# Layer 1's end rearranged: the dense experts' weights in the bias strips' space, batch 6's experts begun earlier, the last head group's tiles two per step

## The reference, cut to what matters

```python
x = x + ga * attn(layernorm(x) * (1 + ca) + sa)        # 16 heads, position bias: "attention 0"
h = layernorm(x) * (1 + cb) + sb
h = h + mla(rmsnorm(h, g1))                            # causal, 16 heads: "attention 1"
t = rmsnorm(h, g2)
top_v, top_i = top_k(t @ gate_w, 2)                    # 8 experts, two per token
gates = softmax(top_v)
hid = silu(einsum('td,edh->teh', t, w1))               # 128 -> 256, each expert
ye = einsum('teh,ehd->ted', hid, w2)                   # 256 -> 128
h = h + sum over the token's two experts of gate * ye
x = x + gb * h
```

## Time and profile before

| | |
|---|---|
| median of 3 runs | 1876.62 us (1873.95 to 1883.99) |
| profiled execution, its own time | 1871.64 us |
| its span, first to last instruction | 1869.9 us |
| mean granted clock of TensorE | 0.947 |
| PE, DVE, ACT, POOL busy | 87%, 71%, 54%, 42% |

### The profile page before, as it was taken

The page is one execution under the profiler, slowest core; times in us unless marked ns, Lnnn a source line. Parts: engine busy times, 40 slices in busy tenths (PEclk is TensorE's granted clock), DMA queues, the critical chain, the costliest instruction groups (busy, mean ns, idle before and its releaser), DMA issues.

```text
span 1869.9 us, 50554 instructions
## 1 busy us (share of the span) xinstructions
PE 1622.4 (87%) x19264; PEld 1184.4 (63%) x19264; DVE 1324.6 (71%) x4176; ACT 1008.1 (54%) x2196; POOL 778.9 (42%) x1021
## 2 busy tenths in 40 slices
PE   3889898899883939999999999989999989878887
PEld 2667776777772727766666666757767667534545
DVE  6678767876761127788778898897877886475646
ACT  1555454555451316665666766656666666454542
POOL 3111211220115237786656576565564563434120
PEclk7899999999995969999999999999999999888999
DMA  4631122122004424344423324243443233535421
GB/s 117 182 94 46 40 84 61 39 69 82 5 8 127 151 91 147 127 151 158 151 85 110 122 96 151 75 142 91 140 142 103 99 126 116 156 95 148 121 64 53
DMA packets 143839, 194.53 MB, mean 104 GB/s; under 512 B 21920, under 2 KB 110176, under 8 KB 142320
## 3 DMA queue, kind: packets, MB, share of 16 engines
q1 hardware_dynamic: 129312, 171.75, 29.5%
q0 software_dynamic: 5760, 14.03, 2.3%
q10 hardware_dynamic: 8528, 5.51, 1.0%
HBM read 142.39 MB, written 50.69 MB: 103 GB/s over the span
## 4 chain that ended last, share of the span: by engine, by line
PE 44%; DVE 10%; issue 6%; ACT 5%; DMA 2%; POOL 1%; SPq 0%; ACTq 0%; another core or an unknown queue 0%; POOLq 0%; DVEq 0%
PE ps L2350 9%; PE ps L2333 7%; PE ps L2384 6%; PE ps L2394 3%; DVE l_XY L2601 3%; PE ps L2361 3%; PE ps L2484 2%; PE ps L2459 2%; ACT PT L2162 2%; DVE ps L2601 2%; PE ps L1229 2%; PE ps L1238 2%; PE ps L2410 1%; PE ps L2431 1%; PE ps L2363 1%
## 5 line engine op out<-in xcount | busy, mean ns | idle before, releaser
L2053 POOL TENSOR_SCALAR l_XY<-l_XY,l_nmax 128x512 f32<-128x512 f32 x512 | 374.3, 736 | 301.7 <-DVE l_nmax L2601 293.5
L2601 DVE CUSTOM_DVE_ANT_0 l_XY<-ps,strips 128x512 f32<-128x512 f32 x512 | 348.0, 687 | 173.4 <-PE ps L2333 115.2
L2162 ACT ACTIVATE PT<-ps 128x512 f32<-128x512 f32 x512 | 307.5, 601 | 244.6 <-PE ps L2350 236.0
L2333 PE MATMUL ps<-l_stack 72*128 72x512 bf16 (+3 forms) x1024 | 351.4, 348 | 54.4 <-DVE l_nmax L2601 39.9
L2350 PE MATMUL ps<-ident,l_XY 128*128 128x128 f32 x2048 | 319.5, 279 | 1.5 <-ACT PT L2162 1.2
L2350 PEld LDWEIGHTS ps<-ident,l_XY 128*128 128x128 f32 x2048 | 235.9, 142 | 89.8 <-issue 56.1
L2601 DVE CUSTOM_DVE_ANT_0 ps<-ps,mask 128x384 f32<-128x384 f32 (+3 forms) x512 | 250.6, 497 | 32.5 <-PE ps L2333 23.3
L2361 PE MATMUL ps<-l_stack 75*128 75x256 bf16 (+3 forms) x512 | 158.6, 311 | 18.6 <-ACT PT_odd L2165 5.8
L2333 PEld LDWEIGHTS ps<-l_stack 72*128 72x128 bf16 x1024 | 101.4, 99 | 105.9 <-DVE l_nmax L2601 61.2
L2384 PE MATMUL ps<-PT,v_aug 128*10 128x128 f32 x4096 | 137.6, 275 | 6.8 <-ACT l_O_sb L2171 6.4
L2165 ACT ACTIVATE PT_even<-ps 128x512 f32<-128x512 f32 (+1 forms) x256 | 125.3, 494 | 24.5 <-PE ps L2363 19.0
(11 more groups left out here) (372 smaller groups left out, 3220.0 us busy)
## 6 DMA issues: line engine op xcount, KB each, us to landing
l_stack<-parts_dram SPq DMA_DIRECT2D x384, 96.0 KB
strips<-bias_dram SPq DMA_DIRECT2D x16, 1792.0 KB
stack<-parts_dram SPq DMA_DIRECT2D x48, 384.0 KB
w_own<-table_dram SPq DMA_DIRECT2D x60, 256.0 KB
parts_dram<-l_parts SPq DMA_DIRECT2D x32, 384.0 KB
rows_dram<-mask SPq DMA_DIRECT2D x6, 2048.0 KB, 9.1
parts_dram<-parts SPq DMA_DIRECT2D x16, 384.0 KB, 6.7
x_b<-rows_dram SPq DMA_DIRECT2D x72, 64.0 KB
```

Of the source, the lines that this page charges most:

```text
L2053: nc.gpsimd.tensor_scalar(XY[:, c % XY_BUFS], XY[:, c % XY_BUFS], -1.0, nmax[:, c % 8:c % 8 + 1], ALU.mult, ALU.add).then_inc(y_pool, 1)
L2162: nc.scalar.activation(PT[:, u % QUADS, j], src.rearrange("p (k q) -> p k q", q=P), ACT.Exp).then_inc(moved, 1)
L2333: nc.tensor.matmul(ps[:, n % 3, 0:w], stack[0:STACK, 0, h, q * P:(q + 1) * P], stack[0:STACK, 1, h, 0:w], start=True, stop=True).then_inc( ...
L2601: nc.vector.tensor_tensor_reduce(out=dst, in0=src, in1=add, scale=-1.0, scalar=3.0e38, op0=ALU.add, op1=ALU.min, accum_out=low).then_inc(s ...
```

## The change

- `strips` is free after step 511, so all eight dense experts' weights go there (`past_strips`) and stay for both batches: eight times two DMAs from ACT, at steps 516, 524, ... 572, counted on one semaphore.
- Batch 6's first expert is at step 12 after MOE_START instead of 18. Its first three experts (APART) keep the rhythm of six steps in banks 6 and 7; from the fourth on they come every four steps, with hidden banks 0 to 2 in turn (ROTATED_FROM), which wait for the last minimum of attention 1. Some router stages are a step earlier.
- The last head group's 16 T tiles (496 to 511) come two per step, from step 658 to 665 instead of 658 to 673; its values, output, divide and turn follow, so batch 7's MOE_START is 675 instead of 684. STEPS is 702 instead of 713.
- Batch 7's logits, top searches and first expert are a step or more closer to its start: the first expert's matmuls are 6 steps after MOE_START instead of 8, in the same step as the logits, and the search for the tops two steps after that.
- COMBINE: batch 4 is added at step 656 instead of 658; batch 5's gathers start at 657 instead of 660 and it is added at 671 instead of 676.

```diff
-T_LAG, B_LAG, MX_AT = 3, 22, 2
+T_LAG, B_LAG, MX_AT, LAST_TURN = 3, 22, 2, 10
+def is_last(a, k):
+    return a == 1 and k == 4 * B - 1
 def turned_step(a, c):
+    if is_last(a, c // GROUP):
+        return begin(a, BIAS) + LAST_TURN + c % GROUP // 2
     return begin(a, c) + (T_LAG, B_LAG)[a] + more(a, c // TILES)
 def values_step(a, u):
+    if is_last(a, u // 4):
+        return turned_step(a, 4 * u + 3) + 2
     return begin(a, 4 * u) + (V_AT, W_AT)[a] + more(a, u // 16)
 def out_step(a, k):
+    if is_last(a, k):
+        return values_step(a, 4 * k + 3) + 2
     return begin(a, GROUP * k) + OUT_AT[a] + more(a, k // 4)
...
-DENSE_STAGES = dict(wo=1, add=3, square=4, power=5, scale=7, turn=10, logits=12, top0=15, top1=16, gap=18,
-                    combine=20, first=18, each=6, second=2, tanh=1, mul=2, ye=9, half=2, sum=2)
-LAST_STAGES = dict(wo=0, add=1, square=2, power=3, scale=4, turn=5, logits=7, top0=9, top1=9, gap=10,
-                   combine=11, first=8, each=2, second=0, tanh=1, mul=1, ye=3, half=0, sum=2)
+DENSE_STAGES = dict(wo=1, add=3, square=4, power=5, scale=7, turn=10, logits=12, top0=14, top1=15, gap=17,
+                    combine=19, first=12, tanh=1, mul=2, sum=2)
+LAST_STAGES = dict(wo=0, add=1, square=2, power=3, scale=4, turn=5, logits=6, top0=8, top1=8, gap=9,
+                   combine=10, first=6, tanh=1, mul=1, sum=2)
+APART = 3
+ROTATED_FROM = APART
...
-COMBINE = {0: (486, 3), 1: (520, 3), 2: (552, 2), 3: (602, 3), 4: (642, 1), 5: (660, 1)}
-COMBINE_ADD, COMBINE_DONE = 9, 10
+EXPERTS_FROM, EXPERTS_EVERY = BIAS + 4, 8
+COMBINE = {0: (486, 3, 9), 1: (520, 3, 9), 2: (552, 2, 9), 3: (602, 3, 9), 4: (642, 1, 7), 5: (657, 1, 7)}
...
 def hidden_at(b, e, f):
-    p = dense(b)
-    return p["first"] + p["each"] * e + p["second"] * f
+    first = dense(b)["first"]
+    if b == B - 1:
+        return first + 2 * e
+    return first + 6 * e + 2 * f if e < APART else first + 6 * APART + 4 * (e - APART) + f
 def ye_at(b, e, u):
-    p = dense(b)
-    return p["first"] + p["each"] * e + p["ye"] + p["half"] * u
+    if b == B - 1:
+        return hidden_at(b, e, 0) + 3
+    return hidden_at(b, e, 0) + (9 + 2 * u if e < APART else 6 + u)
...
-        w1_e = spare[:, 2048:2048 + E_BUFS * F1].rearrange("p (a f) -> p a f", a=E_BUFS)
-        w2_e = spare[:, 3072:3072 + E_BUFS * F1].rearrange("p (a f c) -> p a f c", a=E_BUFS, f=FT1)
+        past_strips = strips[:].rearrange("p h w -> p (h w)")
+        w1_e = past_strips[:, 0:E * F1].rearrange("p (a f) -> p a f", a=E)
+        w2_e = past_strips[:, E * F1:2 * E * F1].rearrange("p (a f c) -> p a f c", a=E, f=FT1)
...
         def hidden_bank(b, e, f):
-            return SIDE + f if b < B - 1 else (2 + FT1 * e + f) % 3
+            n = DENSE.index(b) * E + e - ROTATED_FROM
+            return SIDE + f if n < 0 else (FT1 * n + f) % 3
...
-                def expert(n):
-                    e = n % E
-                    act.dma_start(w1_e[:, n % E_BUFS], w1[e]).then_inc(experts_loaded[n % E_BUFS], 16)
-                    act.dma_start(w2_e[:, n % E_BUFS], w2[e].rearrange("(f p) c -> p f c", p=P)).then_inc(experts_loaded[n % E_BUFS], 16)
-                def first_experts():
-                    act.wait_ge(o_ready, UNIT[0, BIAS // 4 - 1] + 1)
-                    for n in range(E_BUFS):
-                        expert(n)
+                def expert(e):
+                    if e == 0:
+                        act.wait_ge(shifted, NUMBER[0, BIAS - 1] + 1)
+                    act.dma_start(w1_e[:, e], w1[e]).then_inc(experts_loaded, 16)
+                    act.dma_start(w2_e[:, e], w2[e].rearrange("(f p) c -> p f c", p=P)).then_inc(experts_loaded, 16)
...
-                        if i == ye_at(b, e, HALVES - 1) + 1 and n + E_BUFS < len(DENSE) * E:
-                            act.wait_ge(ye_ready, (n + 1) * HALVES)
-                            expert(n + E_BUFS)
...
-                    if m == BIAS + 20:
-                        first_experts()
+                    for e in range(E):
+                        if m == EXPERTS_FROM + EXPERTS_EVERY * e:
+                            expert(e)
...
+                                if n == 0 and f == 0:
+                                    pe.wait_ge(experts_loaded, LOADED_BEFORE + 32 * E)
+                                if e == 0 and f == 0:
+                                    wait_moved(pe, ("xf", b))
+                                if n >= ROTATED_FROM:
+                                    if FT1 * (n - ROTATED_FROM) + f == 0:
                                         pe.wait_ge(shifted, 2 * BIAS)
-                                    elif e >= 1:
+                                    elif FT1 * (n - ROTATED_FROM) + f >= 3:
                                         pe.wait_ge(hid_evac, n * FT1 + f - 2)
...
-                                if b < B - 1 and e < E - 1:
+                                if n + 1 < ROTATED_FROM:
                                     pe.wait_ge(hid_evac, (n + 1) * FT1 + u + 1)
                                 elif n:
                                     pe.wait_ge(ye_added, (n - 1) * HALVES + u + 1)
```

More of the change, by code:

```diff
@@ L1373 @@
 TABLE_AT = TILES + 56
-COMBINE = {0: (486, 3), 1: (520, 3), 2: (552, 2), 3: (602, 3), 4: (642, 1), 5: (660, 1)}
-COMBINE_ADD, COMBINE_DONE = 9, 10
+EXPERTS_FROM, EXPERTS_EVERY = BIAS + 4, 8
+COMBINE = {0: (486, 3, 9), 1: (520, 3, 9), 2: (552, 2, 9), 3: (602, 3, 9), 4: (642, 1, 7), 5: (657, 1, 7)}
 def combine_step(b, stage):
-    first, every = COMBINE[b]
-    return first + {"row": 0, "add": (2 * TT - 1) * every + COMBINE_ADD, "done": (2 * TT - 1) * every + COMBINE_DONE}[stage]
+    first, every, add = COMBINE[b]
+    return first + {"row": 0, "add": (2 * TT - 1) * every + add, "done": (2 * TT - 1) * every + add + 1}[stage]
 def routing(b):
@@ L1417 @@
 STEPS = MOE_START[B - 1] + dense_done(B - 1) + 1
-XY_BUFS, QUADS, E_BUFS, VW = 4, 2, 3, HD + 2
+XY_BUFS, QUADS, VW = 4, 2, HD + 2
 GATHER_AT = 40
@@ L1466, in gather_at @@
     found = []
-    for b, (first, every) in COMBINE.items():
+    for b, (first, every, _) in COMBINE.items():
         part, off = divmod(m - first, every)
@@ L1785, in layer1_phase @@
         y_gathered = sem("y_gathered")
-        experts_loaded = experts.loaded[4:7]
+        experts_loaded = experts.loaded[4]
         table_stored = l1_loaded
@@ L2272, in moe @@
                     p = dense(b)
-                    for e in range(E):
-                        n = DENSE.index(b) * E + e
-                        if i == ye_at(b, e, HALVES - 1) + 1 and n + E_BUFS < len(DENSE) * E:
-                            act.wait_ge(ye_ready, (n + 1) * HALVES)
-                            expert(n + E_BUFS)
                     if i == p["gap"]:
@@ L2492, in moe @@
                             if i == hidden_at(b, e, f):
-                                if f == 0:
-                                    pe.wait_ge(experts_loaded[n % E_BUFS], LOADED_BEFORE + (n // E_BUFS + 1) * 32)
-                                if b == B - 1:
-                                    if e == 0 and f == 0:
-                                        wait_moved(pe, ("xf", b))
+                                if n == 0 and f == 0:
[4 more added lines that the diff above has]
+                                    if FT1 * (n - ROTATED_FROM) + f == 0:
                                         pe.wait_ge(shifted, 2 * BIAS)
-                                    elif e >= 1:
+                                    elif FT1 * (n - ROTATED_FROM) + f >= 3:
                                         pe.wait_ge(hid_evac, n * FT1 + f - 2)
                                 elif e == 0 and f == 0:
-                                    wait_moved(pe, ("xf", b))
                                     pe.wait_ge(o_evac, OUT[1, 4 * CAUSAL_B - 1] + 1)
@@ L2509, in moe @@
                                     pe.wait_ge(ye_added, (n - 2) * HALVES + f + 1)
-                                nc.tensor.matmul(ps[:, hidden_bank(b, e, f), :], w1_e[:, n % E_BUFS, f * P:(f + 1) * P], fT[:],
+                                nc.tensor.matmul(ps[:, hidden_bank(b, e, f), :], w1_e[:, e, f * P:(f + 1) * P], fT[:],
                                                  start=True, stop=True).then_inc(hid_ready, 1)
@@ L2522, in moe @@
                                         last = nc.tensor.matmul(ps[:, SIDE + u, t * C:(t + 1) * C], hid[:, e % 2, f, t * P:(t + 1) * P],
-                                                                w2_e[:, n % E_BUFS, f, :], start=(f == 0), stop=(f == FT1 - 1))
+                                                                w2_e[:, e, f, :], start=(f == 0), stop=(f == FT1 - 1))
                                 last.then_inc(ye_ready, 1)
```

## The result

The changed kernel took 1879.95 us (median of 20 runs; before beside it 1872.9): the ratio is 1.0039, with a 95% interval of 1.0026 to 1.0053, so some 7 us slower. The forecast was a change of -1.3 us. The time lies in the forecast range; the direction was wrong. The profiled execution took 1881.27 us, against 1871.64 before.

The account below looks back on a forecast made before the run. PE, busy 87% of the span, was taken as the bound, with layer 1's idle behind 1787 us. Terms +8.3 - 5.8 - 2.1 - 0.7 - 1.0 = -1.3 us gave 1870.3 (1875 from the median), range 1865 to 1885.

Parts of the forecast that it names:

- the half clock around batch 7's hole: Behind the hole of about 4.9 us ahead of batch 7's normalised rows' turn: logits take 1.2 us at slow clock.
- the price of ACT's pauses and the slow clock ahead of the turn: Steps 658 to 674: ACT's unexplained pauses taken as 1.3 us, half clock behind the 2.6 us hole as 0.9.
- Steps 632 to 657: Layer 1's end, PE full: 6.5 us more PE work plus waits of 1.1 and 0.7; together +8.3 us.
- the hole at pair 35: Step 634: hidden(0,1) writes bank 7, used by block pair 35, so PE waits 1.6 us for ACT and DVE.
- Batch 7, turn to fourth expert: Turn to first expert 10.2 us against 12.3 (-2.1); from there to the fourth expert 10.8 against 11.5 (-0.7).
- Steps 658 to the turn: Last head group up to batch 7's turn: 28.3 us against 34.1, so -5.8 us.
- the bare wait: Step 661: Values 124 waits 1.3 us for bank 5, freed by ACT's copy of head group 30 at step 662.
- the hole of batch 5's sum: Step 671: ye(7,1) on PE waits behind batch 5's sum on DVE; 2.5 us, taken as 2.6.
- The weights: ACT's weight DMAs, steps 516 to 572: -2 for the old burst, +1 for five more pairs; -1 us.
- The end: From batch 7's fourth expert to the end of the span: stays 24.9 us.
- the idle is really filled: Rival, chance 0.2: from step 658 no ACT pauses, slow clock or bank waits, sums beside other work; -9.7 us, 1867.
- two banks bind: Rival, chance 0.11: ACT's exp, exp, tanh stand fully between pairs of T tiles in the last head group; +12, 1888.

Follow-up runs that it names:

- 5: Changed kernel without batch 5's eight gathers on POOL, so batch 5's rows are not computed; made for its trace: ratio 0.999 to before.
- 3: Changed kernel plus five matmuls whose result nobody reads, behind batch 7's output projection: ratio 1.001 to before.
- 6: Changed kernel with batch 5's gathers in their own buffer, set every second step from 650 but run back to back: ratio 1.0049 to before.
- 8: Changed kernel with five unread matmuls behind batch 7's projection, and batch 5's gathers in their own buffer from step 650, without waits: ratio 1.0025 to before.
- 18: The changed kernel unaltered, measured once more on another chip: ratio 1.0033 to before.
- 17: Changed kernel with five unread matmuls and batch 5's gathers paced by waits in their own buffer, measured again on another chip: ratio 1.0004 to before.
- 10: Changed kernel with batch 5's gathers paced by waits in their own buffer, and five unread matmuls behind batch 7's projection: ratio 0.9965 to before.
- 9: Changed kernel with batch 5's gathers in their own buffer, POOL waiting for a T tile ahead of each: ratio 0.9999 to before.
- experiment 1: Kernel before with only the changed kernel's resident expert weights and their issues on ACT: ratio 0.9996 to before.
- 14: Changed kernel with POOL waiting for a T tile ahead of each batch 5 gather, no second buffer, batch 5's sum at step 674: ratio 1.0003 to before.
- experiment 4: Changed kernel with batch 6's last three halves moved behind batch 7's turn and batch 5's sum three steps later: ratio 1.0011 to before.
- kernel 15: Changed kernel with paced gathers in their own buffer, five unread matmuls, and batch 5's sum moved from step 671 to 689: ratio 1.0007 to before.
- 12: Kernel before with resident weights, four unread matmuls behind batch 7's projection, and batch 5's gathers paced in their own buffer: ratio 0.9972 to before.
- 13: Changed kernel with paced gathers, own buffer, five unread matmuls, batch 6's last halves behind batch 7's turn, batch 5's sum at 674: ratio 1.002 to before.
- 16: Changed kernel with paced gathers, own buffer, five unread matmuls, batch 6's last halves behind batch 7's turn, batch 5's sum at 689: ratio 1.0028 to before.

## Why the prediction was wrong

The sum's terms had the right mechanisms; two were mis-sized, both through what stands behind a hole and not through the hole. The step that failed first is the half clock around batch 7's hole, charged to the logits only (1.2 us in all); by experiments 5 and 3 the uncovered hole cost 3.0 us more than a filled one, and with two further falls of the clock after's trace lost 5.9. The second is the price of ACT's pauses and the slow clock ahead of the turn: 2.2 us taken, 6.1 measured.

- **Steps 632 to 657** (+8.3): +7.5. The seven extra matmuls and halves are paid nearly in full (PE is busy 5.8 us longer for 6.5), the hole at pair 35 is 1.68 for 1.6.
- **Batch 7, turn to fourth expert** (-2.1 and -0.7): the failed step. It measured -0.1 and +3.7. The prediction said that the hole "grows from 4.0 to about 4.9 us and covers nothing", and it does; it charged half clock to the logits only (1.2 us). The clock was low from the turn on and stayed so for 17 to 18 us, against 3.4 in before (0.14 of the 12.3 us in the earlier trace rows, twice): against experiment 3, projection +0.9, turn of the normalised rows +0.5, logits +0.8, first hidden records +2.5, and once more +1.6 behind the hole of 1.25 us. The whole is 52.25 - 46.36 = 5.9 us, of which 3.0 belong to the uncovered hole of 4.89 (5 against 3; 2.8 by 6 and 8, 2.7 by 18 and 17). Nearly all of the other 2.9 come of falls at holes of 2.52 and 1.25 us that other traces have without a fall: that after's trace has both is chance as much as the change. With the clock held up, turn to end is 46.3 to 46.4, and the forecast's 10.2 + 10.8 + 24.9 = 45.9 fits. The kernels on after line up by their clock from turn to end: 0.99 and 46.3 (10), 0.93 and 48.0 (8), 0.88 and 49.7 (9), 0.84 and 50.5 (18), 0.80 and 52.25 (after). The Trainium skill (TensorE: Matmul & The Clock Gate, What's actually happening) describes a gate that is closed by default and opened by activity; by that rule idle PE time costs again afterwards, and the four pairs in which idle time was filled with useless work agree (3.7 to 5.5 us in the medians: 3 against after, 8 against 6, 10 against 9, 17 against 18). The prediction named the rule and gave it a span of 1.7 us.
- **Steps 658 to the turn** (-5.8): -2.4. "Two pauses of ACT that nothing in the profile explains" were bounded from 0 to 2.6, taken as 1.3, and the half clock as 0.9. Where pauses occur they cost 24.7 - 20.3 = 4.4 us of PE here (experiments 5 and 9), because in this order ACT's copy l_O_sb, and behind it PE, stands right behind them; Values 124 and the half behind it ran at the slow clock, 1.90 and 1.96 us for 1.05 and 1.16, another 1.7. With these in place of the 2.2 taken, the sum gives 32.2 for the 31.7 measured. The bound was wrong: it took the worst of one arrangement for the worst of all. Everything else fits: the bare wait is 1.31 (1.3), the hole of batch 5's sum 2.52 (2.6).
- **The weights** (-1.0): nothing measurable (experiment 1); the stretch ahead of T470 moved by +1.0 in the trace.
- **The end** (24.9): 24.9.

By these, -0.8, +3.4, +2.0 and +4.4 us in the four stretches, 9.0 in all, are what the forecast missed in the traces, with +2.0 ahead of them for the weights 11.0 in all: +9.7 in the span for -1.3. The medians differ by 7. The time lies in the range only because that is wide: it is 9.7 us above the 1870.3 of the sum and 5 above the 1875 taken from the median. Of the signs of being wrong one came true: batch 7's turn comes at 1827.35, just behind the 1827 that was set. The rival "the idle is really filled" fell: the holes are where the code puts them. So did "two banks bind": outside the named holes PE loses no more than 0.7 us at once between the pairs of T tiles. None of the rivals that had a chance was the clock by itself, and the chance of "slower by over 0.5%" did not contain the mechanism that set the sign.

What stays open: the mechanism of the pauses; whether pacing alone removes them, without the second buffer (14 fell on a chip without pauses); what decides whether the clock falls behind a hole of 1.25 or 2.52 us; why experiment 4's median is as good as 3's; and, but for its hole of 1.74 us, why kernel 15's median is no better than kernel 17's. Kernels 10 and 12 beat before on a chip with pauses, by 0.35% and 0.28%; without pauses 10 is level with before and 0.3% ahead of after, and 12 was not run there.

## What to carry to other kernels

Price a hole in PE by what runs behind it at half clock, not by its length: here a hole of 4.9 us with nothing in it left the clock low for 10 us and more, and cost 3 us in the traces and 3.7 to 5.5 in the medians. Work moved out of a serial chain's shadow must leave enough there, real or useless, to keep PE busy; and a step number is no pace, since an engine that waits for nothing runs all its steps at once. Before believing a gain of a few tenths of a per cent, measure it on more than one chip.

## What the hardware showed that was not expected

- **Useless matmuls pay.** Ten records (4.46 us of PE) in a hole took 2.7 to 3.0 us off the stretch behind it (3 against 5, 8 against 6, 17 against 18), and 3.7 to 5.5 us off the medians, with 10 against 9 as the fourth pair.
- **The clock does not always fall at the same hole.** At the hole of 2.52 us it fell in six of nine traces, and at one of 1.25 us in after, 13, 15 and 16 but not in 3, 5 or 10.
- **ACT and DVE pause beside back-to-back indirect DMAs of POOL.** Eight at 1.3 us: pauses of 2.7 and 3.6 us. Sixteen nearly in a row: 3.9 (ACT) and 6.6 to 8.0 (DVE). At 2.3 us and more between them, behind a wait: none. All 149 pauses of over 0.9 us marked "remote" in the fourteen traces that have them, back to layer 0's bursts of four, end between 0.8 us before and 1.7 us behind the end of an indirect DMA. Spacing alone does not decide it: batch 4's eight gathers in after, 1.3 us apart but for two gaps of 1.7 and 2.6, leave no pause. The DMA engines are not full meanwhile: share 0.29 and 78 GB/s over the eight gathers in after. The Trainium skill (DMA: Bandwidth & Descriptors, SWDGE vs HWDGE vs iDMA) says that for such DMAs GpSimd writes descriptor rings in SBUF, the state that DVE in its 2-port mode locks GpSimd out of. That lock would hold up GpSimd; here GpSimd kept its 1.3 us and DVE and ACT stood, so no run shows it to be the cause.
- **It differs from chip to chip.** In the traces from the chips where before took 1872 to 1874 us (before, after, experiments 1 to 12) ACT and DVE have such pauses in layer 0 and at layer 1's end: 24.5 us in before's trace and 30.5 in after's, added over both engines, which often pause at the same time. In the six traces from the chips where before took 1850 to 1851 us (13 to 18) there is not one. The two traces of the changed kernel, event by event, put the difference at the pauses: the one with pauses is 12.9 us behind after layer 0's last indirect DMA, 9.7 behind at 1579 us, 22.8 at the first of batch 5's gathers and 28.2 at batch 7's turn; between 600 and 1580 us it loses nothing. Each chip was used at one time only, so a lasting property of the chip and a passing one cannot be told apart.
